# Sparse graph attention, second pass: a register for the gathers' highest index, slot counts without range check, and ScalarE waiting for the accumulator in TensorE's place

## The reference

```python
h = jnp.maximum(_layernorm(x, axis=-1), 0.0)
e = jax.nn.leaky_relu(h @ a[:F] + (h @ a[F:]).T, ALPHA)
att = jnp.where(adj > 0, e, NEG_INF)
U = jax.nn.softmax(att, axis=1)
P = 0.5 * U
prop_u = U @ h
rowsum = jnp.sum(U * P, axis=1)
xi = h * rowsum[:, None]
feat = coe[2] * (prop_u - xi) + (1.0 - coe[2]) * (h + prop_u - xi)
feat = jnp.where(jnp.abs(feat) > THRESH, jnp.abs(feat) - THRESH, 0.0) * jnp.sign(feat)
pu = U @ feat
feat_odd2 = feat - coe[3] * pu
feat_even2 = pu + feat_odd2 * rowsum[:, None]
feat_odd2 = coe[0] * feat_odd2 + (1.0 - coe[0]) * h0
out = x + coe[1] * feat_even2 + (1.0 - coe[1]) * feat_odd2
```

## Time and profile before

| | us |
|---|---|
| median of 3 runs | 1500.11 |
| lowest and highest run | 1496.91, 1509.17 |
| the profiled execution's own time | 1488.81 |
| its span, first to last instruction | 1487.2 |

### The profile page before, as it was taken

The page is one execution under the profiler, slowest core; times in us unless marked ns, Lnnn a source line. Parts: engine busy times, 40 slices in busy tenths (PEclk is TensorE's granted clock), DMA queues, the critical chain, the costliest instruction groups (busy, mean ns, idle before and its releaser), DMA issues.

```text
span 1487.2 us, 27559 instructions
## 1 busy us (share of the span) xinstructions
PE 953.7 (64%) x3629; PEld 576.7 (39%) x3630; DVE 932.0 (63%) x5233; ACT 863.0 (58%) x1840; POOL 602.7 (41%) x649
## 2 busy tenths in 40 slices
PE   3545776776676767667777777764266456565665
PEld 2521254443443433333334433332145344343433
DVE  7756556776778878888888888877511222323433
ACT  4673677877788888888888888881222121111111
POOL 1004354443333323322222222215566676666664
PEclk9975689889889888997887787876568777877778
DMA  6989887999999999999999999952344454555665
GB/s 182 358 288 370 335 319 276 336 339 349 353 347 353 378 368 372 371 379 387 374 384 376 366 380 378 371 208 69 87 123 127 120 164 138 162 172 179 191 193 160
DMA packets 146214, 415.70 MB, mean 280 GB/s; under 512 B 29166, under 2 KB 109054, under 8 KB 129782
## 3 DMA queue, kind: packets, MB, share of 16 engines
q1 hardware_dynamic: 115868, 345.65, 62.8%
q0 software_dynamic: 30304, 69.62, 15.0%
HBM read 398.37 MB, written 33.90 MB: 291 GB/s over the span
## 4 chain that ended last, share of the span: by engine, by line
DVE 31%; issue 25%; PE 15%; DMA 6%; another core or an unknown queue 5%; POOL 5%; ACT 4%; POOLq 4%; DVEq 3%; ACTq 1%; SPq 0%
PE TP L321 4%; PE ACC L689 3%; POOL W L634 3%; DVE XHO L1068 2%; PE ACC L693 2%; DMA W<-feat_d,IDT 2%; PE MISC L989 2%; POOLq L623 2%; DMA R<-in_x_dram 1%; ACT SG L309 1%; DMA R<-sc_d 1%; POOL R L634 1%; DVEq L257 1%; DVE JK L1135 1%
## 5 line engine op out<-in xcount | busy, mean ns | idle before, releaser
L309 ACT ACTIVATE SG<-W,ABOVE 128x4096 bf16<-128x4096 f32 x126 | 467.0, 3706 | 77.4 <-DVE cnt L1051 46.9
L634 POOL DMA_INDIRECT R<-haug_d,IDS x230 | 229.8, 999 | 598.2 <-issue 583.0
L321 PE MATMUL TP<-SG,FOLD 128*128 128x512 bf16 x1008 | 304.3, 444 | 0.0
L680 ACT ACTIVATE DG<-ident,WSR 128x128 f32<-128x128 f32 x230 | 76.1, 391 | 338.2 <-remote 181.4
L1777 DVE SCALAR_TENSOR_TENSOR R<-ACC,SELF,R 128x256 f32<-128x256 f32 x63 | 30.5, 484 | 279.3 <-remote 184.1
L688 PE MATMUL ACC<-XHO,ZB 128*128 128x256 bf16 x126 | 40.5, 321 | 217.1 <-ACTq L682 78.5
L634 POOL DMA_INDIRECT W<-feat_d,IDR x140 | 141.4, 1010 | 73.3 <-issue 73.3
L689 PE MATMUL ACC<-R,DG 128*128 128x256 f32 x446 | 162.3, 515 | 1.5 <-issue 1.5
L321 PEld LDWEIGHTS TP<-SG,FOLD 128*128 128x128 bf16 x1008 | 114.6, 122 | 114.4 <-issue 54.5
L689 PEld LDWEIGHTS ACC<-R,DG 128*128 128x128 f32 x446 | 105.0, 252 | 21.6 <-issue 3.0
L688 PEld LDWEIGHTS ACC<-XHO,ZB 128*128 128x128 bf16 x126 | 12.7, 101 | 249.7 <-issue 124.1
(11 more groups left out here) (295 smaller groups left out, 2286.4 us busy)
## 6 DMA issues: line engine op xcount, KB each, us to landing
W<-in_adj_dram SPq DMA_DIRECT2D x128, 2048.0 KB, 13.3
haug_d<-R POOLq DMA_DIRECT2D x8, 1056.0 KB, 9.7
HTS<-haug_d SPq DMA_DIRECT2D x64, 132.0 KB
R<-in_x_dram SPq DMA_DIRECT2D x8, 1024.0 KB, 6.5
R<-feat_d SPq DMA_DIRECT2D x32, 256.0 KB
R<-in_x_dram SPq DMA_DIRECT2D x32, 256.0 KB
R<-in_L_gnn_h_dram SPq DMA_DIRECT2D x32, 256.0 KB
feat_d<-FTS SPq DMA_DIRECT2D x63, 128.0 KB
```

The costliest lines, as they stand in the source:

```text
L309: nc.scalar.activation(SG[:, u, half(h)], W2[:, u, half(h)], ACT.Sign, scale=2.0 ** 100, bias=ABOVE[:], accum_out=DEG[:, u, h:h + 1]).then ...
L321: nc.tensor.matmul(KP[u], FOLD[:, b], SG[:, u, b * FW:(b + 1) * FW], start=False, stop=False)
L634: pool.indirect_dma_start(out=g[:, k, 0:w], out_offset=None, in_=table, in_offset=bass.IndirectOffsetOnAxis(ap=ids[:, k:k + 1], axis=0), * ...
L680: nc.scalar.mul(DG[:, u, k], ident[:], weights[:, k:k + 1])
```

## The change

Three edits, all in the second pass.

1. GpSimd puts N - 1 into a register once, ahead of the loop (`pool.to_reg`), and every gather of the second pass names that register.
2. GpSimd and TensorE load the count of slots with a new helper, `count_of`, that gives no range. `gather_slots` now gets the loaded count from its caller. The first pass and ScalarE keep `slots_of`.
3. ScalarE waits for `out_made` where it waited for `prod2_ready`, TensorE no longer waits for `out_made`, and TensorE's load from `ARR` stands ahead of its wait for `diag2_begun`.

```diff
+        def count_of(eng, t):
+            return eng.value_load(CTL[0:1, bass.ds(t, 1), 0:1].rearrange("a b c -> a (b c)"))
...
-        def gather_slots(pool, t, g, ids, table, w, arrived, others_free=None, **limit):
-
-            slots = slots_of(pool, t)
+        def gather_slots(pool, slots, g, ids, table, w, arrived, others_free=None, **limit):
...
                 act.wait_ge(staged, t + 1)
-                act.wait_ge(prod2_ready, t - 1 + RING)
+                act.wait_ge(out_made, t - 1 + RING)
                 diagonals(act, t, v % 2, WSR[:, v], diag2_begun, diag2_ready)
...
         def second_gpsimd(pool):
+            limit = pool.to_reg(N - 1)
...
-                    gather_slots(pool, t, RINGS[v], IDR[:, v], feat_d, F, gathered2[v], bounds_check=N - 1, oob_is_err=False)
-                gather_tail(pool, RINGS[v], IDT[:, v:v + 1], feat_d, F, gathered2[v], bounds_check=N - 1, oob_is_err=False)
+                    gather_slots(pool, count_of(pool, t), RINGS[v], IDR[:, v], feat_d, F, gathered2[v], bounds_check=limit, oob_is_err=False)
+                gather_tail(pool, RINGS[v], IDT[:, v:v + 1], feat_d, F, gathered2[v], bounds_check=limit, oob_is_err=False)
...
-                slots = slots_of(pe, t)
+                slots = count_of(pe, t)
+                arrived = pe.value_load(ARR[0:1, bass.ds(t, 1)], min_val=16, max_val=16 * KS1 * NT)
                 pe.wait_ge(diag2_begun, t + 1)
-                pe.wait_ge(out_made, t - 1 + RING)
-                pe.wait_ge(gathered2[v], pe.value_load(ARR[0:1, bass.ds(t, 1)], min_val=16, max_val=16 * KS1 * NT))
+                pe.wait_ge(gathered2[v], arrived)
                 first_products(pe, slots, v % 2, RINGS[v])
```

More of the change, by code:

```diff
@@ L897, in body @@
                 pool.wait_ge(ctl_ready, t + 1)
-                gather_slots(pool, t + 1, G[:, u], IDS[:, u], haug_d, AUG, gathered[u], lambda: others_free(t),
+                gather_slots(pool, slots_of(pool, t + 1), G[:, u], IDS[:, u], haug_d, AUG, gathered[u], lambda: others_free(t),
                              bounds_check=N - 1, oob_is_err=False)
@@ L1685, in gather @@
                                         in_offset=bass.IndirectOffsetOnAxis(ap=IDR[:, t, k:k + 1], axis=0),
-                                        bounds_check=N - 1, oob_is_err=False).then_inc(arrived, 16)
+                                        bounds_check=limit, oob_is_err=False).then_inc(arrived, 16)
             def other_gathers(t):
-                slots = slots_of(pool, t)
+                slots = count_of(pool, t)
                 for k in range(S0):
```

## The result

The changed kernel takes 1519.23 us (median of 4 runs, 1513.98 to 1522.33) against 1504.55 for the kernel before in the same comparison (4 runs, 1496.91 to 1509.17): a ratio of 1.0112, 95% interval 1.0074 to 1.0150. The forecast was 1484, the range 1464 to 1503: the measured time lies outside it, on the slow side. The profiled execution after took 1520.73 us with a span of 1519.1. That is 32 us more than the profiled execution of before, but of the medians' 15: the execution of before that was profiled was one of its shortest, so differences between the two traces are to be read at about half their size.

A forecast was written before the change was run, and what follows sets the result against it. GpSimd's gathers were taken to bound the second pass. Savings of 4.8 + 1.5 + 4 + 6.5 = 16.8 us, about 16 after double counting, off the median of 1500.11 gave 1484 us, range 1464 to 1503.

The forecast's parts named there:

- GpSimd as the bound of the second pass: Second pass: GpSimd's 267 gathers at 1.30 us bound it; its idle time beyond 0.30 us a gather, 53 us, counts.
- stretches: Parts of the second pass where sequencer steps take 0.7 us, not 0.03; said to end when GpSimd stands still.
- The sequencer's own part, 0.23 + 0.07 us a stop: GpSimd's long stops: check gone saves 0.23 us, move gone 0.07, over 21 stops 4.8 and 1.5 us.
- No gain between gathers: Between queued gathers the removed move is hidden behind each one's 1.30 us: taken as 0, upper bound 18.7 us.
- I let the short stops fall to half: 4 us of 7.8: GpSimd's 19 short stops (0.38 to 1.3 us) in slow stretches: fewer sequencer steps halve them, saving 4 us.
- Taking 6 of 21 as saved at 2.16 us each ... and half of that given back by stops later: GpSimd's 21 long stops (1.5 to 4.2 us): six avoided save 13 us, half returned by later stops, 6.5 us stay.
- hidden anyway: Rival: skipped GpSimd stops come one tile later at full length, leaving 4 to 6.3 us saved: 1496 us, chance 0.20.
- ScalarE is late: Rival: ScalarE's wait for out_made puts its work behind VectorE's read, lengthening GpSimd's stops: 1518 us, slower, chance 0.13.
- Closer gathers: Rival: the move is part of each gather's 0.30 us, so spacing falls to 1.23 us: 1465 us, chance 0.07.
- the register does nothing: Rival: the move is still issued ahead of each GpSimd gather, so only 9 us are saved: 1491 us, chance 0.05.
- TensorE and ScalarE at 0: Tile start on TensorE: earlier loads against ScalarE's later start sum to +0.1 us, covered by GpSimd's lead: 0, at most 2 us.

The follow-up runs named there:

- the waits alone: Kernel before with only the third edit (ScalarE waits for out_made, TensorE does not, its ARR load stands ahead of its waits): 1493.89 us, ratio 1.0010.
- the drains: Changed kernel with GpSimd waiting until its own queue is empty, ahead of every tile: 1666.6 us (1.1045); ahead of every second tile: 1559.7 us (1.0336).
- lists first: VectorE copies index lists, with their own signal, before reading the accumulator. On the changed kernel: 1.0000, 1390.10 us, 1.0029; on the kernel before: 0.9993, 1391.23 us, 0.9987.

## Why the prediction was wrong

- **GpSimd as the bound of the second pass: right.** On the chips without stretches the pass is nothing but 267 gathers at 1.30 us, 352.0 us from first to last.
- **The sequencer's own part, 0.23 + 0.07 us a stop: right.** 1.47 us from wait to gather became 1.17. Against the growth of a stop, 1.6 us, it is small. I had counted it for all 21 long stops; only 14 of them hold GpSimd's wait at the start of a tile.
- **No gain between gathers: right**, the spacing stays 1.30 us, so the register is worth 0 while work is queued. The Trainium skill ("Advanced Engine Details and Errata", Engine Queue Depths) puts GpSimd's queue at 8 instructions; a sequencer that is ahead of the engine by such a queue would gain nothing by a shorter program, and the unchanged spacing agrees.
- **"I let the short stops fall to half: 4 us of 7.8": the size was off.** They went altogether, 7.2 of 7.8 us. This part of the gain came and was given back.
- **"Taking 6 of 21 as saved at 2.16 us each ... and half of that given back by stops later": this is the step that failed.** 20 of 21 stayed, and they grew from 45.3 to 76.3 us beyond the regular 0.30. I had taken the length of a stop as a constant and its number as what the edit moves. It is the other way round: the number hardly moved, and the kind and length changed. 17 of the 21 stops before ended by GpSimd's own sequencer, 2.3 us each, with the ring not yet empty; 19 of the 20 after ended only when VectorE had read a product and copied lists, 4.3 us each. The stops before were not lost time alone: 20 of the 36 late reads of VectorE fell into them, after each of which it copies the next lists, ahead of need. (The short halts did not do this: one late read in 19 of them.) The rule was in my own text ("They come when GpSimd has gathered without a break for some time, and end when it stands still"), with its outcome ("GpSimd will run on, but only as far as the ring allows, and must stop then"), and I priced that stop at the average of the cheap kind and the dear one. The only stop that I had taken apart was one of 4.03 us, one of the 4 at the ring's end and not of the usual kind; it was the price of what was to come. With the 20 stops at 4.03 instead of 2.46 each, the same sum would have been 31 us worse: 15 us slower in place of 16 faster. That this meets the measured 15 is hindsight and in part luck, as the sum keeps other terms that were off.
- **Of the rivals**, "hidden anyway" was the nearest: "a stop that is skipped comes one tile later at full length". It lacked that full length is longer than the stops there were. "ScalarE is late" named the right side and the wrong cause: the waits alone give 1.0010, and most of the loss is there without them. "Closer gathers" and "the register does nothing" are both out: the spacing is unchanged, and the register alone moves the time by 1.2%, upward.
- **TensorE and ScalarE at 0: right.**

What is shown and what is not: that the loss comes with the slow stretches is shown by the same kernel at 1.0112 and 1.0085 with them and 1.0009 without. The chips could differ in more than the stretches, but on one chip too the kernels that lose are those whose long stops have moved to the ring's end: with the register alone it is all 17. That the signal itself is late is shown by the semaphore's record. With GpSimd halted at each tile the lateness goes, as the drains show. That the earlier, cheaper stops kept the kernel before from the long ones is argued, from the kinds and counts of stops in six kernels, and not tried by itself. What makes the stretches, and why four of the comparisons had them and three, on two chips, had not, stays open. The bytes of the gathers are not it. The Trainium skill ("NOTIFIC — the notification-queue block", §7.1) says that the block that records can hold back its producers; the stretches could be of that sort, and no run here tests it: the changed kernel has 2% fewer recorded instructions (27008 against 27559), and more slow steps on ScalarE and TensorE (178 against 134).

## What to carry over

An idle time on the bounding engine may be what lets the others' signals through. Before pricing a stop as saved, sort the stops by what ends them, ask what is delivered during each, and price the stop that follows by the kind that it will be and not by the average. Run a kernel whose steps or signals show unexplained waits on more than one chip before tuning at it: a loss of 1% came and went with the chip here. Where one engine's copies are all that another waits for, give them a signal of their own ahead of slower work; it took 10 us off the changed kernel where stops were long, and cost nothing where there were none.

## What was unexpected about the hardware

The same kernel took 1491 to 1505 us in four comparisons and 1391 us in three others, on two other chips. The span of the changed kernel differs by 127.3 us (1519.1 to 1391.8). Of these, 75.0 lie in the stretch of gathers (427.0 to 352.0), and 52.8 ahead of the first gather (1082.24 to 1029.42). The large loads of the first pass landed later in the long one of these two executions, as the page's rows of DMA issues show (KB each, median us from issue to landing), of the long execution and then of the short one:

```profile
W<-in_adj_dram SPq DMA_DIRECT2D x128, 2048.0 KB, 13.6
```

```profile
W<-in_adj_dram SPq DMA_DIRECT2D x128, 2048.0 KB, 10.2
```

That is no mark of the chip and not the cause: two other executions without stretches, of 1390.2 and 1389.8 us (lists first on the changed kernel and on the kernel before), have medians of 13.2 and 13.7 us. What lengthens the first pass stays open.

The gathers' spacing, 1.30 us for 128 rows, was the same on all chips, in all kernels, and with a quarter of the bytes. A wait of GpSimd for its own work cost 3.4 us a time, by the difference of the two drain kernels. And a signal whose sender had long been done reached a waiting engine 12 us late (product over at 1286.6, read at 1298.9) while a third engine, GpSimd, was gathering without a break.
